# Two wavefront scans around two attention layers: input, arena and output laid out chunk by chunk, and scan weights made in another order

## What is computed

```
def step(g, inp):
    ci, ni, nm, nc = inp
    local = g[:, ci, :]
    nb = g[:, ni, :]
    neigh = (nb * nm[None, :, None]).sum(axis=1) / nc
    u = jnp.concatenate([local, neigh], axis=-1)
    y_sc = jnp.tanh(u @ w1 + b1) @ w2 + b2
    g = g.at[:, ci, :].set(local + y_sc[:, None] * w_y[None, :])
    return (g, None)
```

## Time and profile before

| | us |
|---|---|
| median of the runs | 4534.51 (4533.5 to 4537.09) |
| the profiled execution | 4535.49 |
| its span, first to last instruction | 4533.4 |
| first scan, about | 0 to 750 |
| attention, about | 750 to 3798 |
| second scan, about | 3798 to 4505 |
| TensorE busy | 4349.7 (96%) |
| VectorE busy | 3476.5 (77%) |
| ScalarE busy | 2842.2 (63%) |
| GpSimd busy | 2267.5 (50%) |

### The profile page before, as it was taken

How to read it: one execution, slowest core, us unless ns; L and a number is a source line. 1 busy time by engine, 2 the same in 40 slices (tenths; PEclk the granted TensorE clock), 3 DMA queues, 4 the chain that set the end, 5 groups by cost and what they waited for, 6 DMA issues and landing times.

```text
span 4533.4 us, 56308 instructions
## 1 busy us (share of the span) xinstructions
PE 4349.7 (96%) x16776; PEld 2252.3 (50%) x16776; DVE 3476.5 (77%) x6544; ACT 2842.2 (63%) x5235; POOL 2267.5 (50%) x3972
## 2 busy tenths in 40 slices
PE   6989996999999999999999999999999999999996
PEld 2446654444444444444444444444444444446754
DVE  5988876777777777777777777777777775898876
ACT  1323322788888888888888888888888884333321
POOL 4654431455555555555555555555555556564431
PEclk9999998899999999999999999999999999999998
DMA  9869419111111122222211111112222221679429
GB/s 165 96 69 109 94 28 67 42 59 60 60 60 56 55 69 70 70 71 71 67 61 59 60 60 60 55 55 67 69 71 71 71 65 33 64 85 121 86 37 47
DMA packets 482495, 309.68 MB, mean 68 GB/s; under 512 B 420624, under 2 KB 432272, under 8 KB 482192
## 3 DMA queue, kind: packets, MB, share of 16 engines
q1 hardware_dynamic: 479088, 305.03, 35.2%
q10 hardware_dynamic: 3104, 1.06, 0.2%
HBM read 137.21 MB, written 135.27 MB: 60 GB/s over the span
## 4 chain that ended last, share of the span: by engine, by line
PE 64%; DVE 9%; ACT 8%; issue 8%; POOL 7%; SPq 2%; DMA 0%; DVEq 0%; POOLq 0%; ACTq 0%
PE psum L1158 14%; PE psum L1078 7%; PE psum L1129 6%; PE psum L1068 6%; PE psum L1092 5%; POOL probs_low L597 4%; PE psum L1142 3%; PE psum L1166 3%; PE psum L1164 3%; PE psum L1163 3%; PE psum L1201 3%; PE psum L1179 3%; PE psum L1188 3%; ACT shared L972 3%; PE psum L1087 3%
## 5 line engine op out<-in xcount | busy, mean ns | idle before, releaser
L597 POOL TENSOR_TENSOR probs_low<-shared,probs_high 128x512 fp32r<-128x512 f32 x1024 | 1307.4, 1277 | 1300.2 <-DVE probs_high L907 1300.2
L869 DVE TENSOR_REDUCE top<-psum 128x1 f32<-128x1024 f32 x1024 | 1253.9, 1225 | 616.1 <-PE psum L1142 615.8
L977 ACT ACTIVATE psum<-psum,top 128x1024 f32<-128x1024 f32 x1024 | 1114.9, 1089 | 279.6 <-DVE top L869 279.6
L972 ACT ACTIVATE shared<-psum 128x512 f32<-128x512 f32 x2048 | 1108.3, 594 | 258.9 <-PE psum L1129 258.8
L1158 PE MATMUL psum<-shared 128*128 128x512 f32 x2048 | 1123.6, 630 | 0.9 <-issue 0.5
L962 ACT ACTIVATE shared<-psum,b_col 128x320 f32<-128x320 f32 (+10 forms) x744 | 413.6, 567 | 1009.5 <-PE psum L1078 995.0
L588 POOL TENSOR_TENSOR shared<-arena 128x32 f32<-128x32 f32 (+6 forms) x1230 | 588.7, 509 | 764.8 <-PE psum L1078 725.2
L1163 PE MATMUL psum<-probs_high,v_high 128*128 128x512 f32 x1024 | 811.5, 792 | 0.0
L1068 PE MATMUL psum<-arena,w_own 128*128 128x320 f32 (+12 forms) x1672 | 539.5, 450 | 21.6 <-DVE w2wy L713 20.8
L1078 PE MATMUL psum<-shared,w_sum 128*128 128x320 f32 (+10 forms) x1488 | 523.3, 474 | 28.7 <-POOL shared L588 13.7
L1129 PE MATMUL psum<-q,k 64*128 64x512 f32 x2048 | 513.2, 497 | 0.3 <-ACT shared L972 0.3
(11 more groups left out here) (115 smaller groups left out, 4455.1 us busy)
## 6 DMA issues: line engine op xcount, KB each, us to landing
layer_out<-x SPq DMA_DIRECT2D x128, 512.0 KB, 2.6
x<-layer_out SPq DMA_DIRECT2D x124, 512.0 KB, 3.3
q<-q SPq DMA_DIRECT2D x256, 128.0 KB, 2.3
arena<-layer_out SPq DMA_DIRECT2D x63, 241.5 KB, 2.4
arena<-x_cells SPq DMA_DIRECT2D x6, 1520.0 KB, 12.3
layer_out<-arena SPq DMA_DIRECT2D x6, 1520.0 KB, 21.1
arena<-layer_out SPq DMA_DIRECT2D x6, 1520.0 KB, 10.9
y_cells<-arena SPq DMA_DIRECT2D x6, 1520.0 KB, 21.4
```

The lines of the kernel that those rows point to most:

```text
L597: nc.gpsimd.tensor_tensor(probs_low[n % 2][:], probs[u % PROBS], probs_high[n % 2][:], ALU.subtract).then_inc(probs_split, 1)
L869: nc.vector.reduce_max(top[i % 2][:, m:m + 1], rows_ps[m % 2][:], AX_X, negate=True).then_inc(row_max, 1)
L972: nc.scalar.activation(probs[u % PROBS], keys_ps[u % 2], ACT.Exp).then_inc(probs_ready, 1)
L977: nc.scalar.activation(rows_ps[m % 2][:], rows_ps[m % 2][:], ACT.Exp, bias=top[i % 2][:, m:m + 1], accum_out=total[i % 2][:, m:m + 1]).the ...
```

## The change

`x_cells` and `y_cells` lie in DRAM as channel, chunk, picture, cell, and the arena in SBUF as chunk, picture, cell. For a chunk of one group, the 32 pictures then lie in one piece per partition on both sides. So a load of the first scan and a store of the second has one run a partition. `layer_out` keeps its layout. The host code in `kernel` makes the new input layout and reads the new output layout. Because the pieces of a picture in the arena are apart now, `refill` issues one DMA for each of the eight chunks, and `fill_last_picture` makes eight copies. In the weights, the multiply of `w1_sum` comes right after its sums, and `b1_col` ahead of `w2_col`; TensorE waits for `w1_own` before its own products, for `w1_sum` before the near ones, and for the rest before the steps; ScalarE waits for `b1_col`.

```
-PLACE = [PLACES[k] + n for k in range(ENDING + 1) for n in range(chunk_size(k))]
+PLACE = [k * CELLS + n for k in range(ENDING + 1) for n in range(chunk_size(k))]
+def chunk_of_images(k, base, first, images):
+
+    n = chunk_size(k)
+    return slice(base + first * n, base + (first + images) * n)
...
-        engine.wait_ge(refilled[g], 32 * (IMAGES - (g == B)))
+        engine.wait_ge(refilled[g], 16 * len(FIRST_LOADS) * (IMAGES - (g == B)))
         if g == B:
-            engine.wait_ge(last_filled, 2)
+            engine.wait_ge(last_filled, len(FIRST_LOADS))
...
-    arena = sb("arena", [P, BATCH, ARENA])
+    arena = sb("arena", [P, BATCH * ARENA])
+
+    def chunk_block(k):
+
+        return arena[:, chunk_of_images(k, BATCH * PLACES[k], 0, BATCH)].rearrange("p (b n) -> p b n", b=BATCH)
+
+    def spot(c, place, w):
+
+        k, n = divmod(place, CELLS)
+        return chunk_block(k)[:, PICTURES[c], n:n + w]
...
-            sp.dma_start(arena[:, PICTURES[g], chunk_places_of(k)],
-                         scan_in[n][PICTURES[g], :, chunk_cells(k)].rearrange("b c n -> c b n")
-                         ).then_inc(loaded[g][k], 16)
+            if n == 0:
+                sp.dma_start(arena[:, chunk_of_images(k, BATCH * PLACES[k], g * IMAGES, IMAGES)],
+                             t["x_cells"][:, chunk_of_images(k, BATCH * chunk_cells(k).start, g * IMAGES, IMAGES)]
+                             ).then_inc(loaded[g][k], 16)
+            else:
+                sp.dma_start(chunk_block(k)[:, PICTURES[g], :],
+                             inner[LAYERS][PICTURES[g], :, chunk_cells(k)].rearrange("b c n -> c b n")
+                             ).then_inc(loaded[g][k], 16)
...
+            if n == 0:
+                sp.dma_start(inner[0][PICTURES[g], :, chunk_cells(k)].rearrange("b c n -> c b n"),
+                             chunk_block(k)[:, PICTURES[g], :]).then_inc(stored[g][k], 16)
+            else:
+                sp.dma_start(t["y_cells"][:, chunk_of_images(k, BATCH * chunk_cells(k).start, g * IMAGES, IMAGES)],
+                             arena[:, chunk_of_images(k, BATCH * PLACES[k], g * IMAGES, IMAGES)]
+                             ).then_inc(stored[g][k], 16)
...
-                sp.dma_start(arena[:, b, first:first + KEPT], inner[LAYERS][b, :, 0:KEPT]).then_inc(refilled[g], 16)
-                sp.dma_start(arena[:, b, chunk_places_of(ENDING)], inner[LAYERS][b, :, chunk_cells(ENDING)]
-                             ).then_inc(refilled[g], 16)
+                for k in FIRST_LOADS:
+                    sp.dma_start(chunk_block(k)[:, b, :], inner[LAYERS][b, :, chunk_cells(k)]
+                                 ).then_inc(refilled[g], 16)
...
-            for w in (w2_col[n], b1_col[n]):
+            dve.wait_ge(weights_turn, turn)
+            nc.vector.tensor_scalar(w1_sum[n][:], w1_sum[n][:], 0.25, None, ALU.mult).then_inc(scan_weights_ready, 1)
+            for w in (b1_col[n], w2_col[n]):
...
+            for k in sorted(FIRST_LOADS):
+                if k == ENDING:
+                    act.wait_ge(out_ready, 2 * i + 2)
+                nc.scalar.activation(chunk_block(k)[:, job_image(i), :], x[i % DEEP][:, chunk_cells(k)], ACT.Copy
+                                     ).then_inc(last_filled, 1)
...
-        act.wait_ge(scan_weights_in[0], 16 * 9)
+        act.wait_ge(weights_turn, 26)
...
             own_products(n, A, 0)
+            pe.wait_ge(scan_weights_ready, n * (2 + HALVES) + 1)
             near_products(n, A, 0)
             own_products(n, B, 0)
+            pe.wait_ge(scan_weights_ready, (n + 1) * (2 + HALVES))
...
-        pe.wait_ge(scan_weights_ready, 2 + HALVES)
+        pe.wait_ge(weights_turn, 14)
```

More of the change, by code:

```diff
@@ L586, in late_sums @@
                     pool.wait_ge(late_ready[c], turn)
-                in0 = out if s0 is None else arena[:, PICTURES[c], s0:s0 + w]
-                nc.gpsimd.tensor_tensor(out, in0, arena[:, PICTURES[c], s1:s1 + w], ALU.add
+                in0 = out if s0 is None else spot(c, s0, w)
+                nc.gpsimd.tensor_tensor(out, in0, spot(c, s1, w), ALU.add
                                         ).then_inc(late_ready[c], 1)
@@ L709, in prepare_scan @@
             larger_first(n)
-            nc.vector.tensor_scalar(w1_sum[n][:], w1_sum[n][:], 0.25, None, ALU.mult).then_inc(scan_weights_ready, 1)
             nc.vector.tensor_tensor(b2wy[n][:], b2wy[n][:], wy_col[n][:], ALU.mult).then_inc(scan_weights_ready, 1)
@@ L764, in old_sums @@
                     dve.wait_ge(near_turn[c], turn_count(n, c, lv) + m)
-                in0 = out if s0 is None else arena[:, PICTURES[c], s0:s0 + w]
-                nc.vector.tensor_tensor(out, in0, arena[:, PICTURES[c], s1:s1 + w], ALU.add
+                in0 = out if s0 is None else spot(c, s0, w)
+                nc.vector.tensor_tensor(out, in0, spot(c, s1, w), ALU.add
                                         ).then_inc(near_turn[c], 1)
@@ L778, in new_sums @@
                     dve.wait_ge(near_turn[c], turn + done)
-                in0 = out if s0 is None else arena[:, PICTURES[c], s0:s0 + w]
-                in1 = arena[:, PICTURES[c], s1:s1 + w]
+                in0 = out if s0 is None else spot(c, s0, w)
+                in1 = spot(c, s1, w)
                 if lv <= WEIGHED:
@@ L823, in update @@
             for o, w, place in own_parts(lv):
-                own = arena[:, PICTURES[c], place:place + w]
+                own = spot(c, place, w)
                 ins = nc.vector.scalar_tensor_tensor(own, columns(step(c, lv), c, lv, o, w), b2wy[n][:], own,
@@ L1022, in fill_first_images @@
                 for k in (ENDING - 1, ENDING):
-                    nc.scalar.activation(x[i][:, chunk_cells(k)], arena[:, i, chunk_places_of(k)], ACT.Copy
+                    nc.scalar.activation(x[i][:, chunk_cells(k)], chunk_block(k)[:, i, :], ACT.Copy
                                          ).then_inc(x_tail, 1)
@@ L1028, in fill_last_picture @@
             i = JOBS - 1
-            first = PLACES[0]
             act.wait_ge(out_ready, 2 * i + 1)
[L1031 to L1035, removed]
+            for k in sorted(FIRST_LOADS):
[3 more added lines that the diff above has]
+                                     ).then_inc(last_filled, 1)
         with nc.allow_non_contiguous_dma(reason="rows to all partitions"):
@@ L1068, in own_products @@
                     nc.tensor.matmul(columns(pre(c, lv, h), c, lv, o, w), w1_own[n][:, tile(h)],
-                                     arena[:, PICTURES[c], place:place + w], start=(m == 0), stop=False,
+                                     spot(c, place, w), start=(m == 0), stop=False,
                                      skip_group_check=True)
@@ L1253 @@
     x = arrays.pop("x").reshape(BATCH, CELLS, P)[:, GRID, :]
-    arrays["x_cells"] = np.ascontiguousarray(x.transpose(0, 2, 1))
+    arrays["x_cells"] = np.concatenate([x[:, chunk_cells(k), :].transpose(2, 0, 1).reshape(P, -1)
+                                        for k in range(NC)], axis=1)
     for n in ("L0_conv_b2", "L3_conv_b2", "L1_conv_gamma"):
@@ L1258 @@
     t = {n: nc.dram_tensor(n, a.shape, F32, kind="ExternalInput").ap() for n, a in arrays.items()}
-    t["y_cells"] = nc.dram_tensor("y_cells", [BATCH, P, CELLS], F32, kind="ExternalOutput").ap()
+    t["y_cells"] = nc.dram_tensor("y_cells", [P, BATCH * CELLS], F32, kind="ExternalOutput").ap()
     build(nc, t)
@@ L1262 @@
     y = np.empty((BATCH, CELLS, P), np.float32)
-    y[:, GRID, :] = got.transpose(0, 2, 1)
+    for k in range(NC):
+        part = got[:, chunk_of_images(k, BATCH * chunk_cells(k).start, 0, BATCH)]
+        y[:, GRID[chunk_cells(k)], :] = part.reshape(P, BATCH, chunk_size(k)).transpose(1, 2, 0)
     return y.reshape(BATCH, SIDE, SIDE, P)
```

7 lines of the change are left out of this document (removed).

## The result

The changed kernel takes 4507.49 us (4506.52 to 4508.46) against 4534.58 us (4533.5 to 4537.09) for the kernel before, run beside it: ratio 0.994, 95% interval 0.9928 to 0.9952. It is faster, by 27.1 us; 42.5 had been forecast, and 4507.49 lies 1.5 us outside the range. The span of the profiled execution is 4505.7 us (4533.4 before).

A forecast was written before the change was run, and what follows sets the result against it. TensorE and ScalarE pace the middle; transfers hold the engines at the start, before attention and at the end. From the profiled 4535.49 us, 18.3 (start) and 24.5 (end) come off: 4492.7, 4492 as a median; range 4479 to 4506.

The forecast's parts named there:

- I take the present 13.26, since both queues carry the same bytes: At the start, the last of nine weight loads still lands at 13.26 us; part of the 18.3 us start gain.
- late-weights rival: At the start, weight loads take turns with SP's loads one for one, landing at 23.5; time 4502; chance 0.14.
- The lower bound of the weights: At the start, unhindered weights land at 4.65 + 1.6 = 6.3 us, giving 6 us more gain.
- The cells: In the first scan's loads, A's level 0 chunks are there at 8.9 us and B's at 17.1.
- old-rate rival: Loads and stores stay at 209 GB/s, limited by something other than run length; time 4501; chance 0.08.
- The pace after the first step: In the first scan, near (A, 0) to (A, 4) takes the second scan's 40.94 us, not 51.80; 10.9 us gained.
- The end: After the last update, the second scan's last stores land sooner and the span ends at 4508.9; 24.5 us gained.
- The weights' order alone: At the start, the new order of making the weights, with the loads as they were, would be worth nothing.
- The costs taken at nothing: More refill issues (2.3 us on SP), seven copies for the last picture (1.9 us) and new arena pitch cost nothing.
- the pitch: New arena spacing between pictures costs nothing; as rival it slows scan accesses, 4535 or above; chance 0.03.
- More is gained: Between first scan and attention, contiguous arena side shortens `layer_out` DMAs and the queries' wait, at most 18 us, 4474; chance 0.10.
- the refills' rival: In attention, eight refill DMAs a picture delay the swap or shift rows past their reader; 4594 if fully exposed; chance 0.03.

The follow-up runs named there:

- Old stores: The changed kernel with `y_cells` and the second scan's stores as before the change (4,096 runs each): 4531.8 us, ratio 0.9994.
- old loads: The changed kernel with `x_cells` and the first scan's loads as before the change: 4505.22 us, ratio 0.9938.
- short runs: The changed kernel with `x_cells` laid out so each first-scan load has eight runs a partition, 448 to 1,536 B, instead of one: 4499.06 us, ratio 0.9924.
- hold B: The changed kernel with SP waiting for the nine weight loads after issuing A's first three chunks: 4494.64 us, ratio 0.9916.
- hold part two: The changed kernel with SP waiting for the nine weight loads before it loads chunks 3 to 6: 4500.92 us, ratio 0.9928.

## Why the prediction was wrong, point by point

- *The step that failed* is "I take the present 13.26, since both queues carry the same bytes". It is the last weight landing, and it measured 30.94. The bytes of both queues were the same, but the size of one packet on SP's queue was not, and that sets how long ScalarE's 97 packets take. Without the term's 17.7 us the near products of (A, 0) would have started at 20.0, by the sum; at 37.65 the start gained 1.7 us in place of 18.3. That is 16.6 us; the total missed by 15.5.
- *The late-weights rival* had the right cause and the wrong size. It took nine loads' turns (23.5 us, time 4502); the turns go by packet (638 to 638). I had quoted the rule of the Trainium skill, "DMA: Bandwidth & Descriptors", "Queues, rings and completion order", that each DMA engine goes round the queues by whole packets, and then worked out the rival by whole loads. The trace agrees in part: the engines do go round the two queues, and not by whole loads. But where the section gives about 9 to 17 descriptors as typical of a packet, a turn here is one packet of the profile, a single run of a load, and beside short runs the counts weren't one to one. Worked out afterwards, 1,552 packets of weights beside as many of SP's of 6.2 KB on average (10.21 MB in 1,649) are 10.2 MB, the weights' own 0.6 included, and 29 us at the 349 GB/s of that stretch (10.81 MB in 31 us).
- *The lower bound of the weights*, 6.3, was a load of 0.1 KB applied to the ninth of nine. Alone on the engines the set lands at 10.89.
- *The cells* were right: 8.99 and 17.35 for 8.9 and 17.1. The engines moved 349 GB/s on average over the first 31 us, above the 309 taken, so the old-rate rival is out.
- *The pace after the first step* was right and even slightly better: from (A, 0) to (A, 4) 77.63 - 37.65 = 39.98 us where 40.94 stood, so the late transfers did go, and with them 51.80 - 39.98 = 11.8 us. 10.2 of these were spent on the later start.
- *The end* was right: 24.7 for 24.5, stores landing in 2.5 to 4.0 us. Old stores shows that it is all of the gain that can be told from no change.
- *The weights' order alone is worth nothing*: right with the old loads; with the new ones it is worth 4.35 us.
- *The costs taken at nothing* held. Refills now issue for 3.66 us a picture, but the swaps still follow each other at 23.39 us (2213.61 to 2237.00), as in the earlier trace rows. The seven copies end 2.15 us before the half that they share the tile with is ready:

```profile
3793.84 1.16 ACT L1053 ACTIVATE arena<-x 128x32 f32<-128x32 f32 x7
...
3797.15 0.23 ACT L1053 ACTIVATE arena<-x 128x28 f32<-128x28 f32 x1 [2.15 <-DVE x L946]
```

  The updates of levels with 15 cells, to be read against the earlier trace rows, did not change either, so the pitch costs them nothing:

```profile
L845 DVE SCALAR_TENSOR_TENSOR arena<-psum,b2wy,arena x9: 714/719/719, 132.7 to 168.0; 128x480 f32<-128x480 f32 x9
```

- *More is gained* didn't come: the wait for the swapped queries is 21.16 where it was 20.40.
- *A slip in the refills' rival:* 145 us lost on a forecast of 4492 give 4637. The 4594 takes the gain of 42.8 off a second time. The refills cost nothing, so the result doesn't depend on it.

What stays open is small. Attention differs by up to 3 us between executions (3021.96 us in old loads to 3024.7 in short runs, 3023.86 before), and no run here says why.

## What to carry to other kernels

When one queue's transfers get longer runs, look at every other queue that shares its DMA engines: beside runs of 3.5 to 12 KB the small loads here took turns with them packet by packet, so count their packets and multiply by the time of one long one. Beside short runs that product comes out too low: two or three of the other queue's packets passed for each. Put the small, early ones ahead of the long ones on the same queue, which gave a ratio of 0.991 here instead of 0.994, or cut the long runs finer; that gave 0.9924 with all of them cut, and cutting only those beside the small loads was not tried. And price each part of a change by undoing it alone; here one of three parts held all of the gain that could be measured.

## What the runs showed of the hardware

- With one run of several KB a partition on SP's queue, the two queues' packets stood one to one (638 to 638; 2,104 to 2,075). With the old runs of 112 to 376 B, in the kernel before, it was 5,304 of SP's to 1,696 of ScalarE's up to 13.3 us, three to one; with runs of 448 to 1,536 B it was 3,661 to 1,841 up to 15.4 us, two to one. So the turns are not one to one at every size, and a forecast from one size doesn't hold at another. Why the ratio changes no run shows.
- The weight set's landing by what shares the engines: nothing 10.89 us, on SP's queue ahead of the cells 11.45, runs of 112 to 376 B 13.26 and 15.16, of 448 to 1,536 B 15.38, of 3.5 to 12 KB 30.94.
- The last four stores (two of 608 KB, two of 448) land in 2.5 to 4.0 us as 128 runs each, and in 16.7 to 30.7 as 4,096 runs of 152 and 112 B.
- VectorE's making of `w1_own`, the same instructions each time, takes 3.1 us when GpSimd's sums don't overlap it (30.94 to 34.07; 3.1 in hold B too) and 6.3 (short runs) and 5.7 (hold part two) when they do.
